# A decoder layer's attention: one of two head pairs has its probabilities parted into f16 and turned by DMA transposes

## The chip, the cores and the metric

One core of a Trainium2 chip runs the whole layer in one launch. The metric is device time in microseconds of one execution, here the median of three runs. The core's engines work from queues of their own and meet at semaphores: TensorE (products and transposes, into PSUM), ScalarE, VectorE, GpSimd, and SyncE, which here only issues DMAs.

## The reference, cut to what matters

The layer has causal self-attention, a cross-attention with three recurrent steps, and a mixture of eight experts. The change is in the first. `x` is (8, 256, 256) in f32, there are 16 heads of 64.

```python
q = (x @ Wq).reshape(N, S, HEADS, HEAD_DIM).transpose(0, 2, 1, 3)
k = (x @ Wk).reshape(N, S, HEADS, HEAD_DIM).transpose(0, 2, 1, 3)
v = (x @ Wv).reshape(N, S, HEADS, HEAD_DIM).transpose(0, 2, 1, 3)
logits = jnp.einsum('nhid,nhjd->nhij', q, k) * scale
causal = 1000000000.0 * (jnp.tril(jnp.ones((S, S), dtype=logits.dtype)) - 1.0)
attn = jax.nn.softmax(logits + causal[None, None, :, :], axis=-1)
out = jnp.einsum('nhij,nhjd->nhid', attn, v)
out = out.transpose(0, 2, 1, 3).reshape(N, S, HEADS * HEAD_DIM)
return out @ Wo + bo
```

## The kernel before, in words

Attention is cut into 32 double steps (STAGES), four to each of the eight batches. A double step has two pairs of heads, p = 0 and p = 1. The projections run as f16 products on operands parted in two: a high half (the value cast to f16) and a low half (what is left), and three products, high x high, high x low and low x high (`HILO`, `split_matmuls`). Scores, the transposes of the probabilities and the weighing of the values are f32. An f32 product of scores and of the weighing shows as two passes in the trace, so 24 rows for 12 products.

All engines run the same loop over j, from -2 to 32, and each has its own fixed order in it. In iteration j TensorE computes the scores of step j+1, weighs the values of step j-1, projects queries and keys of step j+2 (its first pair), does a share of the preparation of the cross-attention, transposes the probabilities of step j (`turn_prob`), projects the output of step j-1, then the second pair of queries and keys (`queries_keys` evicts them) and the values of step j+1. The shares differ: none before j = 8, four transposes from 8 on, f32 products from 18 to 25, four transposes again from 26.

VectorE adds the mask and finds the maxima (`masks`), ScalarE takes the exponentials, GpSimd multiplies by the reciprocal sums (`normalise`), TensorE turns the result in PSUM, and VectorE (pair 0) and ScalarE (pair 1) copy it to `pT` (`probs_turned`). With each step go 36 weight pieces of the experts, a filler for ScalarE (`piece_high`, 2, 1, 2, 0 of them in four iterations), VectorE (`piece_low`, in shares, at three places of an iteration) and SyncE, which loads a piece and stores its halves (`piece_load`, `piece_store`). A buffer holds three pieces. In iterations 4 to 7 ScalarE also squares the context.

SyncE's queue is in the order of the text of `attention_sync`: inputs, attention weights, three pieces, ten context loads, two stores of zeros (`rows_x`, `back_y`), then the loads and stores of the pieces. PSUM bank 1 holds the values of step j until ScalarE has evicted them (`values_out`); then the weighing of step j-1 writes there. That is why the weighing waits for `v_out`.

Of the kernel before, what the change touches and what calls it, by code (L numbers as in the profile page):

```python
# [34 lines left out]
def decoder_layer(nc, a, out):  # L35
# [23 lines left out]
    with top:  # L59
# [58 lines left out]
        def constants_pool():  # L118
# [12 lines left out]
            PO.memset(zrow[:, :], 0.0).then_inc(const_fill, 1)  # L131
# [200 lines left out]
        def vw_tensor(i):  # L332
# [8 lines left out]
            elif i == 1:  # L341
                PE.wait_ge(qk_out, ITEMS)
            elif i < 4:
                PE.wait_ge(pT_out, 2 * STAGES)
            else:
                PE.wait_ge(o_hi, STAGES)
                PE.wait_ge(o_lo, STAGES)
# [109 lines left out]
        p_out = [sem(f"p_out{u}") for u in range(STAGED)]  # L457


        with ExitStack() as c:  # L460
            wo = [sb(c, f"wo{i}", [P, PAIRS, D], F16) for i in range(2)]
            bo = sb(c, "bo", [P, D])
            zrow = sb(c, "zrow", [P, D + 2])
# [17 lines left out]
            w_in = [sem(f"w_in{i}") for i in range(4)]  # L481
            x_in = [sem(f"x_in{i}") for i in range(3)]
# [6 lines left out]
                sem(k) for k in ("recip", "normed", "pT_out", "o_hi", "o_lo"))  # L489
            y_added, y_stat, y_rstd, y_out = (sem(k) for k in ("y_added", "y_stat", "y_rstd", "y_out"))  # L490
# [7 lines left out]
            FIRST, LAST = -2, STAGES  # L498
            X_EARLY = 2
# [103 lines left out]

            def attention_sync():
# [17 lines left out]
                SY.dma_start(rows_x[0:P, :], zrow[:, :]).then_inc(zeroed, 16)  # L622
# [18 lines left out]
            def attention_pool():  # L641
                def normalise(m, p):
                    u = m % 2
                    PO.wait_ge(recip, 2 * m + p + 1)
                    for h in (2 * p, 2 * p + 1):
                        for t in range(2):
                            r = query_tile(t)
                            PO.tensor_scalar(prob[u][:, h, r], prob[u][:, h, r], rden[u][:, h, t:t + 1],  # L648
                                             1.0, ALU.mult, ALU.mult).then_inc(normed, 1)
# [12 lines left out]
                for j in range(FIRST, LAST + 1):  # L662
                    if j >= 0 and j % DOUBLES == 0 and j // DOUBLES < NB:
                        add_bias(j // DOUBLES)
                    if 0 <= j + 1 < STAGES:
                        normalise(j + 1, 0)
                        normalise(j + 1, 1)
                    if batch_ending(j) is not None and j < LAST:
# [10 lines left out]
            def attention_tensor():  # L679
# [13 lines left out]
                def turn_prob(m):  # L693
                    for p in range(2):
                        if m + 1 < STAGES:
                            PE.wait_ge(masked, 8 * (m + 1) + 4 * (p + 1))
                        PE.wait_ge(normed, 8 * m + 4 * (p + 1))
                        for h in (2 * p, 2 * p + 1):
                            for blk in range(3):
                                mm = PE.transpose(ps[:, 2 + h, blk * P:blk * P + P],  # L700
                                                  prob[m % 2][:, h, blk * P:blk * P + P], ident[:, :])
                        mm.then_inc(p_turned, 1)
# [18 lines left out]
                def scores(m):  # L721

                    if m >= 2:
                        PE.wait_ge(pT_out, 2 * (m - 1))
                    for p in range(2):
                        PE.wait_ge(qk_out, 2 * m + p + 1)
                        for t in range(2):
# [6 lines left out]
                def weigh_values(m):  # L734
                    PE.wait_ge(pT_out, 2 * (m + 1))
                    PE.wait_ge(v_out, min(m + 2, STAGES))
                    for p in range(2):
                        for t, key, at in ((0, 0, 0), (1, 0, P), (1, 1, 2 * P)):
                            for h in range(2):
                                r = slice(HD * h, HD * h + HD)  # L740
                                mm = PE.matmul(ps[r, 1, (2 * p + t) * P:(2 * p + t) * P + P], v_sb[m % 2][:, key, p, r],  # L741
                                               pT[:, 2 * p + h, at:at + P], start=key == 0, stop=key == t,
                                               skip_group_check=True)
# [1794 lines left out]
```

## Time and profile before

| | us |
|---|---|
| median of 3 runs | 889.33 |
| lowest, highest | 887.21, 890.68 |
| the profiled execution | 890.64 |
| its span, first to last instruction | 889.4 |
| TensorE busy in the span | 859.9 (97%) |
| VectorE busy | 606.1 (68%) |
| ScalarE busy | 557.2 (63%) |
| GpSimd busy | 377.8 (42%) |

The span is what the trace covers, and its times count from the first instruction. The mean granted TensorE clock is 0.996 of full. The double steps take the time from about 16 to 357 us. In rows of the timeline the first number is the start, the second the time from it to the end of the group, then engine, line, operation, output and input, shape, and the count; in brackets the idle time before and who ended it. TensorE's products overlap, so the start of the next group says more than the length of one.

### The profile page before, as it was taken

What the parts mean: (1) busy time and instruction counts of PE and PEld (TensorE: products, weight loads), DVE (VectorE), ACT (ScalarE), POOL (GpSimd) and SP (SyncE); (2) the same over time, 40 slices, a digit from 0 to 9 for tenths busy, and PEclk for the clock granted to TensorE, in tenths of its full rate; (3) what the DMA queues carried; (4) which work ended last, traced back from release to release, by engine and by line L of the source; (5) the groups of instructions that cost most, each with busy time, mean ns of one, the idle gap of its engine ahead of it and who ended that gap; (6) DMA issues with size and microseconds to landing.
All of it is one profiled execution on the core that took longest, in us unless ns stands there. A gap on an engine that the chain in (4) does not pass through costs nothing. (4 is left out here: it accounts for less than half of the span.)

```text
span 889.4 us, 23089 instructions
## 1 busy us (share of the span) xinstructions
PE 859.9 (97%) x8094; PEld 680.0 (76%) x8094; DVE 606.1 (68%) x1669; ACT 557.2 (63%) x1251; POOL 377.8 (42%) x492
## 2 busy tenths in 40 slices
PE   5999999999999999999999999999999999999996
PEld 3888788888888888767676666676788888887864
DVE  3667588776667675756666667869677767766655
ACT  4988776777676776655756565564455555555555
POOL 1634354343433475324444332544534444444433
PEclk9999999999999999999999999999999999999999
DMA  9733424342424331410000000399423323333226
GB/s 317 207 126 113 142 97 152 119 160 96 143 94 138 103 119 49 62 42 2 1 1 1 2 1 1 105 393 356 158 52 50 49 44 50 49 50 50 43 27 195
DMA packets 61579, 88.04 MB, mean 99 GB/s; under 512 B 17279, under 2 KB 46527, under 8 KB 61343
## 3 DMA queue, kind: packets, MB, share of 16 engines
q1 hardware_dynamic: 53439, 75.52, 25.8%
q0 software_dynamic: 7488, 10.27, 7.3%
q8 instruction: 71, 1.16, 0.6%
q10 hardware_dynamic: 544, 0.79, 0.3%
q14 instruction: 37, 0.30, 0.1%
HBM read 56.00 MB, written 30.56 MB: 97 GB/s over the span
## 5 line engine op out<-in xcount | busy, mean ns | idle before, releaser
L648 POOL TENSOR_SCALAR prob<-prob,rden 128x128 f32<-128x128 f32 (+1 forms) x256 | 122.9, 498 | 183.1 <-DVE rden L949 183.0
L2219 PE MATMUL ps<-slots,e 128*128 128x128 f16 x1872 | 190.0, 219 | 2.2 <-DVE xs L2386 2.1
L2219 PEld LDWEIGHTS ps<-slots,e 128*128 x1872 | 152.6, 97 | 35.3 <-issue 4.4
L843 ACT ACTIVATE prob<-prob,nmx 128x128 f32<-128x128 f32 (+1 forms) x256 | 113.2, 444 | 29.8 <-DVE nmx L943 29.8
L2227 PE MATMUL ps<-e,xT 128*128 x312 | 117.3, 378 | 0.0
L2316 ACT ACTIVATE slots<-slots 128x512 f32<-128x512 f32 x78 | 49.1, 630 | 106.8 <-DVE slots L2370 106.8
L943 DVE CUSTOM_DVE_ANT_0 prob<-ps,mask 128x128 f32<-128x128 f32 (+1 forms) x256 | 73.7, 353 | 41.5 <-PE ps L730 41.5
L31 PE MATMUL ps<-xT,wqkv 128*128 128x256 f16 x768 | 97.2, 278 | 2.0 <-ACT slots L850 1.4
L31 PEld LDWEIGHTS ps<-xT,wqkv 128*128 128x128 f16 x768 | 73.4, 99 | 18.3 <-issue 6.9
L1731 POOL DMA_INDIRECT xg<-rows_x,dst x39 | 40.9, 1049 | 106.3 <-DVE mask L2359 103.0
L2228 PE MATMUL ps<-e,xT 128*128 x312 | 85.0, 273 | 0.0
L2375 DVE TENSOR_TENSOR xT<-slots,xT 128x1024 f16<-128x1024 f32 x39 | 47.8, 1225 | 39.9 <-ACT xT L2322 39.9
L2191 POOL DMA_INDIRECT back_y<-xs,dst x39 | 62.2, 1595 | 29.8 <-DMA back_y<-xs,dst 16.7
L2370 DVE SCALAR_TENSOR_TENSOR slots<-ps,b1e 128x512 f32<-128x512 f32 x78 | 53.7, 691 | 26.5 <-PE ps L2219 26.3
L592 DVE SCALAR_TENSOR_TENSOR parted<-piece,parted 128x256 f16<-128x256 f32 x144 | 59.8, 463 | 0.0
L31 PE MATMUL ps<-an,wqkv 120*128 120x256 f16 x432 | 58.9, 272 | 0.5 <-POOL an L1477 0.5
L730 PE MATMUL ps<-slots 64*128 64x128 f32 (+1 forms) x512 | 53.1, 345 | 2.5 <-ACT slots L850 2.5
L31 PEld LDWEIGHTS ps<-an,wqkv 120*128 120x128 f16 x432 | 41.2, 99 | 16.5 <-POOL an L1477 2.5
L31 PE MATMUL ps<-wst,whh 128*128 128x512 f16 x216 | 52.5, 379 | 0.0
L31 PE MATMUL ps<-s,whh 128*128 128x512 f16 x216 | 52.5, 379 | 0.0
L956 DVE COPY pT<-ps 128x768 f32<-128x768 f32 x32 | 30.6, 956 | 31.8 <-PE ps L700 31.8
L741 PEld LDWEIGHTS ps<-pT,v 128*64 128x64 f32 x768 | 42.4, 139 | 11.5 <-issue 11.5
(267 smaller groups left out, 1855.3 us busy)
## 6 DMA issues: line engine op xcount, KB each, us to landing
halves<-parted SPq DMA_DIRECT2D x36, 512.0 KB, 2.9
piece<-in_L_ffn_ew SPq DMA_DIRECT2D x32, 512.0 KB, 4.5
e<-halves SPq DMA_DIRECT2D x16, 1024.0 KB, 15.2
piece<-in_L_ffn_sh_w SPq DMA_DIRECT2D x4, 512.0 KB, 8.8
sw<-halves SPq DMA_DIRECT2D x4, 512.0 KB, 6.8
rows_x<-xs SPq DMA_DIRECT2D x4, 512.0 KB, 7.4
xs<-back_y SPq DMA_DIRECT2D x8, 256.0 KB, 4.4
out<-xs SPq DMA_DIRECT2D x8, 256.0 KB, 2.1
```

Source lines behind the costliest of these rows:

```text
L31: mm = pe.matmul(out, w, x, start=first and n == 0, stop=last and n == len(products) - 1, **kw)
L592: VE.scalar_tensor_tensor(share(piece_part(q, 1)), share(like_part(q)), WS, share(piece_part(q, 0)), ALU.mult, ALU.subtract).then_inc(p_lo, 1)
L648: PO.tensor_scalar(prob[u][:, h, r], prob[u][:, h, r], rden[u][:, h, t:t + 1], 1.0, ALU.mult, ALU.mult).then_inc(normed, 1)
L730: mm = PE.matmul(ps[:, 2 + 2 * p + h, query_tile(t)], qk[p][r, 0, t * P:t * P + P], qk[p][r, 1, 0:(t + 1) * P], start=True, stop=True)
L843: SC.activation(at, at, ACT.Exp, bias=nmx[u][:, h, t:t + 1], scale=-1.0, accum_out=den[u][:, h, t:t + 1]).then_inc(exped, 1)
L943: VE.tensor_tensor_reduce(prob[u][:, h, r], ps[:, 2 + h, r], mask[:, r], -SCALE, HIGHEST, ALU.add, ALU.min, nmx[u][:, h, t:t + 1]).then_in ...
L2191: PO.indirect_dma_start(back_y, bass.IndirectOffsetOnAxis(ap=dst[:, i:i + 1], axis=0), yo[i % 2], None, compute_op=ALU.add).then_inc(rows_ ...
L2219: yield PE.matmul(ps[:, 2 * u + q, (k % 4) * P:(k % 4) * P + P], w[ch][h], xgT[u][j][:, ch, :], start=n == 0, stop=n == 3 * DC - 1)
L2227: yield PE.matmul(ps[:, 4 + u, :], he[u][0][:, k, :], w, start=k == 0, stop=False, skip_group_check=True)
L2228: yield PE.matmul(ps[:, 4 + u, 0:D], he[u][1][:, k, :], w[:, 0:D], start=False, stop=k == IC - 1, skip_group_check=True)
L2316: SC.activation(z, z, ACT.Gelu_apprx_tanh).then_inc(U_gelu, 1)
L2370: VE.scalar_tensor_tensor(z, ps[:, 2 * u + q, :].rearrange("p (k t) -> p k t", k=4), 1 / WS, bias, ALU.mult, ALU.add).then_inc(U_bias, 1)
```

## The change

The probabilities of pair 0 are no longer turned by TensorE. ScalarE casts them to f16 (`probs_high`, the high half), GpSimd subtracts that from the f32 value (`probs_low`, the low half, times 4096 both), and SyncE issues one DMA transpose of the 128x1536 f16 block into `pT_parts` (`turn_parts`). The values of pair 0 are parted as well: ScalarE writes the high half, VectorE the low one (`values_low`), scaled by 8. TensorE weighs them in three f16 products in place of one f32 product, three key blocks by two heads by three, 18 in all. The heads' eviction divides by 4096 x 8. Pair 1 stays f32 as it was, and its turned probabilities are copied by ScalarE alone. `p_parts`, the source of the transpose, is one buffer; `pT_parts` is two. SyncE's loop is written in the order of the iterations now, with each transpose at the second of three places. `bo`, `zrow`, the f32 values and some semaphores share storage with others.

```diff
@@ PSUM and SBUF
-            v_sb = [sb(c, f"v{i}", [P, S // P, 2, P]) for i in range(2)]
+            v_sb = [v.rearrange("p (k n) -> p k n", n=P) for v in (xg[:, 1, 0:S], part(wst[0], 4 * DC * G3, S))]
+            v_parts = [[sb(c, f"v{i}_{h}", [P, S // P, P], F16) for h in range(2)] for i in range(2)]
-            pT = sb(c, "pT", [P, 4, 384])
+            pT = sb(c, "pT", [P, 2, 384])
+            p_parts = sb(c, "p_parts", [P, 2, 2, 384], F16)
+            pT_parts = [sb(c, f"pT_parts{u}", [P, 2, 2, 3, P], F16) for u in range(2)]
@@ SyncE
+            def turned_parts(engine, m):
+                engine.wait_ge(parts_turned[m % 2], 16 * (m // 2 + 1))
+            def turn_parts(m):
+                SY.wait_ge(prob_lo, m + 1)
+                if m >= 2:
+                    SY.wait_ge(o_mm, m - 1)
+                SY.dma_start_transpose(
+                    out=pT_parts[m % 2][:, :, :, :, :].rearrange("p i h k q -> p (i h k) q"),
+                    in_=p_parts[:, :, :, :].rearrange("p i h n -> p (i h n)")).then_inc(parts_turned[m % 2], 16)
...
-                for q in range(PIECES + STAGED - 1):
-                    if PIECES_EARLY <= q < PIECES:
-                        piece_load(q)
-                    if q >= STAGED - 1:
-                        piece_store(q - STAGED + 1)
+                for j in range(-1, STAGES):
+                    for place in range(3):
+                        if place == 1 and j + 1 < STAGES:
+                            turn_parts(j + 1)
+                        for n in low_shares.get((j, place), ()):
+                            if n % LOW_SHARES == LOW_SHARES - 1:
+                                if n // LOW_SHARES + STAGED < PIECES:
+                                    piece_load(n // LOW_SHARES + STAGED)
+                                piece_store(n // LOW_SHARES)
@@ GpSimd, after normalise(j + 1, 0) and normalise(j + 1, 1)
+                def probs_low(m):
+                    PO.wait_ge(prob_hi, m + 1)
+                    PO.tensor_tensor(p_parts[:, 1, :, :], prob[m % 2][:, 0:2, :], p_parts[:, 0, :, :],
+                                     ALU.subtract).then_inc(prob_lo, 1)
@@ TensorE
-                    for p in range(2):
-                        if m + 1 < STAGES:
-                            PE.wait_ge(masked, 8 * (m + 1) + 4 * (p + 1))
-                        PE.wait_ge(normed, 8 * m + 4 * (p + 1))
-                        for h in (2 * p, 2 * p + 1):
...
+                    PE.wait_ge(normed, 8 * (m + 1))
+                    for h in (2, 3):
...
-                    PE.wait_ge(pT_out, 2 * (m + 1))
                     PE.wait_ge(v_out, min(m + 2, STAGES))
...
+                    PE.wait_ge(v_lo, min(m + 2, STAGES))
+                    turned_parts(PE, m)
+                    for blk, (t, key) in enumerate(((0, 0), (1, 0), (1, 1))):
+                        for n, (i, j) in enumerate(HILO):
+                            for h in range(2):
+                                r = slice(HD * h, HD * h + HD)
+                                PE.matmul(ps[r, 1, t * P:t * P + P], v_parts[m % 2][i][:, key, r],
+                                          pT_parts[m % 2][:, j, h, blk, :], start=key == 0 and n == 0,
+                                          stop=key == t and n == len(HILO) - 1, skip_group_check=True)
+                    PE.wait_ge(pT_out, m + 1)
@@ ScalarE; probs_high(j + 1) stands between the pieces and queries_keys(2 * (j + 2) + 1)
+                def probs_high(m):
+                    SC.wait_ge(normed, 8 * m + 4)
+                    if m >= 1:
+                        turned_parts(SC, m - 1)
+                    SC.copy(p_parts[:, 0, :, :], prob[m % 2][:, 0:2, :]).then_inc(prob_hi, 1)
...
-                    SC.mul(v_sb[m % 2][:, :, :, :], ps[:, 1, :].rearrange("p (t m n) -> p t m n", t=2, m=2),
-                           1 / WS).then_inc(v_out, 1)
+                    SC.mul(v_sb[m % 2], v[:, 1, :, :], 1 / WS).then_inc(v_out, 1)
+                    SC.mul(v_parts[m % 2][0][:, :, :], v[:, 0, :, :], V_UP / WS).then_inc(v_hi, 1)
@@ VectorE; values_low(j) stands first in the iteration, ahead of the masks
-                def probs_turned(m):
-                    VE.wait_ge(p_turned, 2 * m + 1)
-                    if m >= 1:
-                        VE.wait_ge(o_mm, m)
-                    VE.tensor_copy(pT[:, 0:2, :], ps[:, 2:4, 0:384]).then_inc(pT_out, 1)
+                def values_low(m):
+                    VE.wait_ge(v_hi, m + 1)
...
+                    VE.scalar_tensor_tensor(v_parts[m % 2][1][:, :, :], v, V_UP / WS, v_parts[m % 2][0][:, :, :], ALU.mult,
+                                            ALU.subtract).then_inc(v_lo, 1)
```

TensorE's queue before, over iteration 2: scores (L730), weighing (L741), queries and keys, transposes (L700), output projection (wo), queries and keys.

```order
L730 MATMUL ps<-slots 128x128 x2
L730 MATMUL ps<-slots 128x256 x2
L741 MATMUL ps<-pT,v 64x128 x12
L31 MATMUL ps<-xT,wqkv 128x256 x12
L700 MATMUL ps<-ident,prob 128x128 x12
L31 MATMUL ps<-wo,oT 128x256 x12
L31 MATMUL ps<-xT,wqkv 128x256 x12
```

The same place of the changed kernel; v_0 and v_1 are the high and low halves of the values, pT_parts the transposed halves of the probabilities.

```order
L761 MATMUL ps<-slots 128x128 x2
L761 MATMUL ps<-slots 128x256 x2
L773 MATMUL ps<-pT_parts,v_0 64x128 x4
L773 MATMUL ps<-pT_parts,v_1 64x128 x2
L773 MATMUL ps<-pT_parts,v_0 64x128 x4
L773 MATMUL ps<-pT_parts,v_1 64x128 x2
L773 MATMUL ps<-pT_parts,v_0 64x128 x4
L773 MATMUL ps<-pT_parts,v_1 64x128 x2
L780 MATMUL ps<-pT,wst 64x128 x6
L31 MATMUL ps<-xT,wqkv 128x256 x12
L729 MATMUL ps<-ident,prob 128x128 x6
L31 MATMUL ps<-wo,oT 128x256 x12
```

Six transposes of twelve are gone, six f32 products of the weighing stay, and 18 f16 products stand ahead of them. SyncE's queue before, from the last context loads on:

```order
L163 DMA nw<-in_L_xattn_input_norm_w 128x2x1
L163 DMA nw<-in_L_xattn_slot_norm_w 128x2x1
L622 DMA rows_x<-zrow 128x258
L623 DMA back_y<-zrow 128x256
L602 DMA halves<-parted 128x2048
L598 DMA piece<-in_L_ffn_sh_w 128x4x256
```

And of the changed kernel:

```order
L163 DMA nw<-in_L_xattn_input_norm_w 128x2x1
L163 DMA nw<-in_L_xattn_slot_norm_w 128x2x1
L641 DMA rows_x<-xg 128x258
L642 DMA back_y<-xg 128x256
L619 DMA_TRANSPOSE pT_parts<-p_parts 128x12x128 x4
L605 DMA piece<-in_L_ffn_sh_w 128x4x256
L609 DMA halves<-parted 128x2048
```

The transposes of steps 0 to 3 stand behind the context loads and the two stores of zeros, and ahead of the first piece's load. ScalarE's queue around the end of an iteration, before:

```order
L857 COPY pT<-ps 128x768
L582 ACTIVATE parted<-piece 128x1024
L834 ACTIVATE wo<-wst 128x512
L850 ACTIVATE slots<-ps 128x512
L863 ACTIVATE v<-ps 128x512
L843 ACTIVATE prob,den<-prob,nmx 128x128
```

And of the changed kernel (L904 is the high half, L913 and L914 the values):

```order
L897 COPY pT<-ps 128x768
L589 ACTIVATE parted<-piece 128x1024
L874 ACTIVATE wo<-wst 128x512
L904 CAST p_parts<-prob 128x768
L890 ACTIVATE slots<-ps 128x512
L913 ACTIVATE wst<-ps 128x256
L914 ACTIVATE v_0<-ps 128x256
L883 ACTIVATE prob,den<-prob,nmx 128x128
```

The high half stands ahead of the queries and keys (L890), and one eviction of the values has become two.

## Rows read from the trace of the kernel before

**Rows 1.** The page, chain that ended last: share of the span by engine.

```profile
PE 33%; DVE 2%; issue 1%; POOL 1%; ACT 1%; DMA 0%; DVEq 0%; POOLq 0%; ACTq 0%
```

**Rows 2.** Waits from 40 to 345 us: total, times, longest.

```profile
ACT parted L582 <- DMA piece<-in_L_ffn_ew: 6.1, 6, 1.9
...
PE ps L730 <- ACT slots L850: 2.0, 2, 1.8
```

**Rows 3.** Timeline of TensorE, iteration 10: start, length, group.

```profile
125.31 1.58 PE L730 MATMUL ps<-slots 64*128 64x128 f32 x16
126.82 1.53 PE L741 MATMUL ps<-pT,v 128*64 128x128 f32 x24
128.29 1.48 PE L31 MATMUL ps<-xT,wqkv 128*128 128x256 f16 x12
...
130.04 1.47 PE L700 MATMUL ps<-ident,prob 128*128 128x128 f32 x12
131.35 1.47 PE L31 MATMUL ps<-wo,oT 128*128 128x256 f16 x12
132.66 1.47 PE L31 MATMUL ps<-xT,wqkv 128*128 128x256 f16 x12
...
135.38 1.58 PE L730 MATMUL ps<-slots 64*128 64x128 f32 x16
```

**Rows 4.** Timeline of ScalarE, iteration 10.

```profile
125.42 0.60 ACT L863 ACTIVATE v<-ps 128x512 f32<-128x512 f32 x1 [0.67 <-PE ps L31]
126.97 0.40 ACT L843 ACTIVATE prob<-prob,nmx 128x128 f32<-128x128 f32 x1 [0.95 <-DVE nmx L943]
...
130.97 0.57 ACT L850 ACTIVATE slots<-ps 128x512 f32<-128x512 f32 x1
131.55 0.80 ACT L857 COPY pT<-ps 128x768 f32<-128x768 f32 x1
132.25 1.06 ACT L582 ACTIVATE parted<-piece 128x1024 f16<-128x1024 f32 x1
134.17 0.60 ACT L850 ACTIVATE slots<-ps 128x512 f32<-128x512 f32 x1 [0.86 <-PE ps L31]
```

**Rows 5.** Timeline of SyncE's queue, end of the context loads.

```profile
38.53 1.00 SPq L163 DMA_DIRECT2D nw<-in_L_xattn_slot_norm_w  x1
...
40.08 0.43 SPq L623 DMA_DIRECT2D back_y<-zrow  x1
```

**Rows 6.** Timeline of TensorE, first expert tile: products without others between.

```profile
637.75 4.23 PE L2219 MATMUL ps<-slots,e 128*128 128x128 f16 x48
```

**Rows 7.** Timeline of VectorE, first mask of iteration 10.

```profile
126.28 0.29 DVE L943 CUSTOM_DVE_ANT_0 prob<-ps,mask 128x128 f32<-128x128 f32 x1 [0.82 <-PE ps L730]
```

**Rows 8.** Groups of GpSimd: busy us, mean ns, idle before.

```profile
L655 POOL TENSOR_TENSOR xs<-xs,bo 128x512 f32<-128x512 f32 x8 | 10.5, 1308 | 0.0
```

**Rows 9.** Timeline at the start of iteration 1, ScalarE and TensorE.

```profile
31.47 0.58 ACT L850 ACTIVATE slots<-ps 128x512 f32<-128x512 f32 x1
31.84 1.58 PE L730 MATMUL ps<-slots 64*128 64x128 f32 x16
```

**Rows 10.** DMA issues: count, KB each, median us to landing.

```profile
halves<-parted SPq DMA_DIRECT2D x36, 512.0 KB, 2.9
...
bih<-in_L_xattn_gru_bih SPq DMA_DIRECT2D x1, 3.0 KB, 10.0
```

**Rows 11.** Timeline of TensorE, starts of iterations 4, 9, 18 and 26.

```profile
61.16 0.93 PE L730 MATMUL ps<-slots 64*128 64x128 f32 x8
...
114.81 1.58 PE L730 MATMUL ps<-slots 64*128 64x128 f32 x16
...
206.76 1.58 PE L730 MATMUL ps<-slots 64*128 64x128 f32 x16
...
297.56 1.58 PE L730 MATMUL ps<-slots 64*128 64x128 f32 x16
```

**Rows 12.** Busy time and clock (PEclk) of a stretch after the longest stall.

```profile
104.50:107.50 3.00, 3.00 (x28) 2.42 (x24) 1.96 (x11) 1.50 (x8) 0.44 (x2) 0.50 0.00 0
```

More of the change, by code:

```diff
@@ L489, in decoder_layer @@
                 sem(k) for k in ("recip", "normed", "pT_out", "o_hi", "o_lo"))
+            v_hi, v_lo, prob_hi, prob_lo = (sem(k) for k in ("v_hi", "v_lo", "prob_hi", "prob_lo"))
+            parts_turned = [sem(f"parts_turned{u}") for u in range(2)]
             y_added, y_stat, y_rstd, y_out = (sem(k) for k in ("y_added", "y_stat", "y_rstd", "y_out"))
@@ L498, in decoder_layer @@
             FIRST, LAST = -2, STAGES
+            P_UP, V_UP = 4096.0, 8.0
+            O_UP = P_UP * V_UP
             X_EARLY = 2
@@ L693, in turn_prob @@
                 def turn_prob(m):
-                    for p in range(2):
-                        if m + 1 < STAGES:
-                            PE.wait_ge(masked, 8 * (m + 1) + 4 * (p + 1))
-                        PE.wait_ge(normed, 8 * m + 4 * (p + 1))
-                        for h in (2 * p, 2 * p + 1):
[L699 to L702, printed above, removed]
+                    if m + 1 < STAGES:
+                        PE.wait_ge(masked, 8 * (m + 2))
+                    PE.wait_ge(normed, 8 * (m + 1))
+                    for h in (2, 3):
+                        for blk in range(3):
+                            mm = PE.transpose(ps[:, 2 + h, blk * P:blk * P + P],
+                                              prob[m % 2][:, h, blk * P:blk * P + P], ident[:, :])
+                    mm.then_inc(p_turned, 1)
                 def project_qk(n):
@@ L721, in scores @@
                 def scores(m):
-                    if m >= 2:
-                        PE.wait_ge(pT_out, 2 * (m - 1))
+                    if m >= 1:
+                        PE.wait_ge(masked, 8 * m)
                     for p in range(2):
                         PE.wait_ge(qk_out, 2 * m + p + 1)
+                        if p == 1 and m >= 2:
+                            PE.wait_ge(pT_out, m - 1)
                         for t in range(2):
@@ L852, in probs_turned @@
                 def probs_turned(m):
[L854 removed]
+                    SC.wait_ge(p_turned, m + 1)
                     if m >= 1:
                         SC.wait_ge(o_mm, m)
[L857 removed]
+                    SC.copy(pT[:, :, :], ps[:, 4:6, 0:384]).then_inc(pT_out, 1)
+                def probs_high(m):
+                    SC.wait_ge(normed, 8 * m + 4)
+                    if m >= 1:
+                        turned_parts(SC, m - 1)
+                    SC.copy(p_parts[:, 0, :, :], prob[m % 2][:, 0:2, :]).then_inc(prob_hi, 1)
                 def values_out(m):
@@ L870, in heads_high @@
                         SC.wait_ge(y_mm, (b - 1) * SHARES + slot // 2 + 1)
-                    SC.copy(oT[0][:, slot:slot + 2, :].rearrange("p s q -> p (s q)"), ps[:, 1, :]).then_inc(o_hi, 1)
+                    SC.mul(oT[0][:, slot:slot + 2, :].rearrange("p s q -> p (s q)"), ps[:, 1, :],
+                           1 / O_UP).then_inc(o_hi, 1)
                 inputs_high(0)
@@ L1717, in decoder_layer @@
                 sem(k) for k in ("U_mm", "U_bias", "U_gelu", "U_hi", "U_lo", "D_mm", "D_out"))
-            gathered = [sem(f"gathered{q}") for q in range(NT // 2)]
             f_stat, f_rstd, f_norm, f_late, stored = (
@@ L2419, in late_low, with combine_loaded @@
                 VE.tensor_tensor(hh[m % 3][1], hf[m % 2], hh[m % 3][0], ALU.subtract).then_inc(H_late, 1)
+            def combine_loaded(engine, q):
+                engine.wait_ge(loaded[q], 32 if q < len(w_in) + len(x_in) else 16)
             def combine_load(engine, q):
                 rows = back_y[P + q * CT * P:P + (q + 1) * CT * P, :].rearrange("(t p) d -> p t d", p=P)
-                engine.dma_start(xs[:, q * CT:(q + 1) * CT, :], rows).then_inc(gathered[q], 16)
+                engine.dma_start(xs[:, q * CT:(q + 1) * CT, :], rows).then_inc(loaded[q], 16)
             def combine_sync():
```

50 lines of the change are left out of this document (29 added, 21 removed).

## The prediction

> **What bounds the kernel now.** I read the page first, then the waits, then one iteration in order of time. TensorE has 33% of the span in the chain that ended last, the next engine 2% [rows 1]; over the attention stage it waited for another engine only twice [rows 2]. So the 32 double steps cost what TensorE's queue costs. One of them, iteration 10 in the loop over j, runs from 125.31 to 135.38: 10.07 us, of which scores take 1.51, the weighing 1.47 (126.82 to 128.29) and the twelve transposes 1.31 (130.04 to 131.35) [rows 3]. ScalarE in the same iteration starts the values' eviction at 125.42, the first exponential at 126.97, has exponentials and the heads' copy done at 130.97, copies pT, parts a weight piece, and then waits 0.86 us for TensorE [rows 4]. Its idle time is about 3 us in 10, so it is the next engine in line. SyncE's queue is the other place to look at: it is still issuing the context loads when the double steps are under way, and is free only at 40.08 + 0.43 = 40.51 [rows 5].
>
> **The change, part by part.** The profiled run took 890.64 us (span 889.4), 1.3 above the median 889.33; I sum on 890.6.
>
> *TensorE.* Six of twelve transposes go: 1.31 / 2 = 0.655 us per iteration. Of the 24 f32 passes of the weighing 12 stay (0.735). The other 12 become 18 f16 products of 64 columns. Now a pass takes 61 ns (1.47 / 24), since the two heads write different column halves side by side. No f16 product in halves is in the trace. Bounds: 48 f16 products of the same 128 columns over the whole array take 4.23 us, 88 ns each [rows 6]; if halves do not overlap, 18 x 88 = 1.58. An f16 product of 256 columns takes 109 ns (131.35 to 132.66 for twelve) [rows 3], so 128 columns in two halves side by side could go at 27 ns, 0.49 in all. I take 48 ns, a little above 88 halved and below the 61 of the pass that it replaces: 0.87 us. So an iteration bound by TensorE goes from 10.07 to 10.07 - 0.655 - 0.735 + 0.87 = 9.55: a gain of 0.52 (bounds 0.90 and -0.19).
>
> The Trainium skill (TensorEngine Tiling (Array Packing), "Restrictions") says that column tiling switches the fast weight load off. By it the 18 loads would be slower than those of the 128-column products, the cost would lie in the upper half of my bounds, and the gain per iteration would be near zero, which makes the sum some 10 us longer; no row shows such an f16 load, so I leave it in the bounds.
>
> *ScalarE.* It gets the high half of the probabilities, 128x768, and two evictions of 256 columns for one of 512. The 768-element copy of pT occupies it 0.70 us (131.55 to 132.25) [rows 4]; the same for the new one. The two evictions push the parted values' end from 0.6 to about 0.66 after their start, then VectorE needs 0.46 for the low half, all ahead of the masks: these now start 0.86 us after the eviction (126.28) [rows 7], then about 1.15. The first exponential moves from 1.55 to 1.85 after it. With nothing to wait for, an iteration of ScalarE is then 1.85 + 4.00 (exponentials and heads) + 0.48 + 0.70 (pT) + 0.70 (new) + 0.50 (last queries and keys) = 8.23 us, plus 0.96 per weight piece. Pieces per iteration go 2, 1, 2, 0 in turn, the inputs' copy adds 0.48 once in four, and a piece that isn't there yet added 6.1 us over six times [rows 2]. Over four iterations: 32.9 + 4.8 + 0.5 + 0.8 = 39.0 us, against TensorE's 4 x 9.55 + 0.44 = 38.6, and unevenly placed (10.6 beside 10.0, then 11 beside 9.6). I put four at 39.6 instead of 40.7: 0.28 gained per iteration, not 0.52. Behind the new copy in ScalarE's queue stand the queries and keys for which scores wait, so its lateness lands on TensorE at once.
>
> *VectorE* loses the pT copy (0.96) and gains 0.46. *GpSimd* gains a subtraction over 128x768: 1.31 x 768 / 512 = 1.96 us [rows 8], in a queue that idles more than that. Both are covered.
>
> *SyncE and the transfer.* The first transpose, T(0), stands behind all context loads, so it can't be issued ahead of 40.51. Two instructions wait for it: the weighing of step 0, and ScalarE's high half of step 1 (the buffer of parts is single), behind which stand the queries and keys that ran at 31.47 and let the second half of scores go at about 32.6 [rows 9]. No transpose is in the trace. Bounds for issue to landing: 2.9 us for a 512 KB store in large rows, 10.0 for a load in 4-byte elements [rows 10]. The probabilities are 384 KB in 256-byte rows; I take 4.0, near the first. It lands at 44.5; then 0.8 for the high half, 0.6 for queries and keys: scores go on at 45.9 instead of 32.6. Start: **+13.3** (bounds 12.2 and 19.3). Later ones are issued when the low half is done, about 1 us into an iteration, and wanted 6.9 us later by ScalarE (an iteration of 9.7 less 0.7 for the high half, 1.96 for the low one and 0.1): hidden.
>
> The Trainium skill puts a crossbar transpose at 261 GB/s (DMA: Bandwidth & Descriptors, "Latency and other measured facts"), which with the 2 us of fixed cost in its section on the anatomy of one DMA is an estimate of 3.5 us: by it the sum would be 0.5 us less. No run yet shows it.
>
> *The sum by stages* (starts in [rows 3, 9, 11]):
> Start: +13.3.
> Iterations 1 to 3: now 61.16 - 31.84 = 29.3. ScalarE also scales output weights (0.55 each): 3 x 8.23 + 5 x 0.96 + 1.65 + 0.5 + 0.8 = 32.4: +3.1. TensorE's slow clock after the long stall lies beside this.
> Iterations 4 to 8: now 53.65, with the longest stall, 1.8, and a granted clock of 0.50 behind it [rows 2, 12]. ScalarE also squares the context (1.07 in each of four): 9.3 + 11.7 + 10.3 + 13.0 + 9.6 = 53.9, and I add 1: +1.2.
> 9 to 17: 9 x 0.28 = -2.5.
> 18 to 25: 11.35 each ((297.56 - 206.76) / 8), with f32 products of the preparation that leave ScalarE room: 8 x 0.52 = -4.2.
> 26 to 31: 6 x 0.28 = -1.7.
> Together +9.2: **900 us**. Its own range is 892 to 910.
>
> **Rivals.**
> *The transfer is slow.* High half (0.7), low half (1.96), issue (0.1) and landing L follow one another and must fit an iteration of 9.7: it decides from L = 6.9. For it: many short rows; against it: large transfers land in 2.9. With the far row, L = 10.0, a period is 12.8; 31 of them take 397 against 327 now (10.56 each), +70, and the start +19: about 978. The Trainium skill (VectorE: DVE Perf Modes, "The three transpose paths") has 1309 ns for one block of 128x128; twelve in a row would be an estimate of 15.7 us. As a mechanism of this kernel, blocks that go one by one, each double step would take 18.5 us and the time beyond 1100. I give this form 0.05 of the 0.23 below.
> *Loads of pieces come late.* SyncE's queue now holds the load that follows a transpose until the low half is there. For it: the late piece that already stopped TensorE for 1.8 us and was followed by half the clock [rows 2, 12]; against it: such loads have an iteration of slack. Eight such stalls of 1 us more and half of them with the slow clock: +8 + 4 x 1.7 = +15, 915.
> *Not slower.* One mechanism: the side-by-side halves go at 27 ns and ScalarE's idle 3 us takes all that is new, so each of 31 iterations gains 0.90 (28 us), against 12.2 + 1 at the start: 876. It decides from a gain of 0.42 per iteration on. Against it is the ScalarE sum of 39.0 for four. At a gain of 0.4 the time is that of before.
>
> **How the numbers follow.** Forecast 0.48; late pieces 0.12; slow transfer 0.23; not slower 0.17, of it 0.09 faster and 0.08 the same. A difference under 0.5% (4.4 us) is no change for a measurement of this kernel. So faster 0.09, same 0.08, slower 0.83. The range leaves out the gain below 889 and the slowest transfers: 889 to 980.
>
> **What would show it.** Right: TensorE idle for about 13 us from 32.6 on, ended by a DMA or ScalarE; the transpose issued at 40.5; the 18 products in 0.87 us; iterations of about 9.9 from 9 to 17 and 10.8 from 18 to 25. Wrong: a landing above 6.9 us, and TensorE or ScalarE waiting for it in every iteration; products at 88 ns; or a first transpose well ahead of 40 us.

## The result

| | us |
|---|---|
| before, median of 5 runs beside it | 888.42 (886.57 to 890.68) |
| after, median of 5 runs | 948.64 (947.51 to 955.58) |
| ratio | 1.0689, 95% interval 1.0651 to 1.0727 |
| the profiled execution of after, its span | 955.58, 954.3 |
| mean granted clock of TensorE | 0.961 (0.996 before) |

The change costs 60 us. A cost of 10 was forecast, in a range of 889 to 980. The profiled execution is the slowest of the five, 7 us above the median, so the waits and stages read from it below are a little larger than those of a median one.

The page of the changed kernel, busy time of TensorE and the chain that ended last:

```profile
PE 859.9 (90%) x8094; PEld 664.2 (70%) x8094; DVE 595.2 (62%) x1669; ACT 583.1 (61%) x1315; POOL 434.6 (46%) x524
...
PE 30%; DVE 2%; issue 1%; POOL 1%; ACT 1%; DMA 0%; DVEq 0%; POOLq 0%; ACTq 0%
```

TensorE is busy for 859.9 us, to the tenth what it was before. So the whole 64.9 us by which the span grew (889.4 to 954.3) are idle TensorE. That the busy time stays the same hides two things: less work, and a slower clock. The chain has hardly changed [rows 1]: it names TensorE, and doesn't show where the time went. The waits do. From 14 to 430 us (engine, line, what it waited for: total, times, longest):

```profile
POOL p_parts L677 <- ACT p_parts L904: 93.2, 27, 11.5
...
PE ps L761 <- ACT slots L890: 56.9, 15, 13.4
ACT parted L589 <- DMA halves<-parted: 45.4, 24, 3.6
...
ACT p_parts L904 <- DMA pT_parts<-p_parts: 12.7, 1, 12.7
```

Scores wait for queries and keys 56.9 us in 15 stalls. The same line of the kernel before, over the same stretch:

```profile
PE ps L730 <- ACT slots L850: 2.5, 3, 1.8
```

So 54.4 of the 64.9 us are this wait. One of the stalls is the start, 13.4. The others go with a wait that the kernel before did not have: ScalarE, about to write the high half of a weight piece into `parted`, waits for the *store* of the piece that was there, 24 times.

The DMA issues (KB each, median us from issue to landing):

```profile
halves<-parted SPq DMA_DIRECT2D x36, 512.0 KB, 5.6
...
pT_parts<-p_parts SPq DMA_TRANSPOSE x32, 3.8
```

Transposes land in 3.8 us. The stores land in 5.6, where they took 2.9 [rows 10].

Starts of iterations in both traces [rows 11 for before] give the time by stages:

| iterations | before | after | longer | forecast |
|---|---|---|---|---|
| 1 to 3, with the start | 29.32 | 46.17 less 0.87 (earlier begin) | 16.0 | 16.4 |
| 4 to 8 | 53.65 | 70.78 | 17.1 | 1.2 |
| 9 to 17 | 91.95 | 106.40 | 14.5 | -2.5 |
| 18 to 25 | 90.80 | 99.85 | 9.1 | -4.2 |
| 26 to the end | 591.84 | 600.13 | 8.3 | -1.7 |

The first stage is as forecast; the error lies in the 28 iterations behind it. Iterations of 9.9 us from 9 to 17 and of 10.8 from 18 to 25 were to show that the prediction was right; they take 11.8 and 12.5. Here is one such place in four engines' own order (start, length, group, in brackets the idle time before it and what ended it). SyncE's queue while TensorE is in iterations 7 and 8:

```profile
121.52 1.42 SPq L619 DMA_TRANSPOSE pT_parts<-p_parts  x1
122.98 0.89 SPq L605 DMA_DIRECT2D piece<-in_L_ffn_ew  x1
123.91 0.44 SPq L609 DMA_DIRECT2D halves<-parted  x1
124.40 0.43 SPq L605 DMA_DIRECT2D piece<-in_L_ffn_ew  x1
124.87 1.34 SPq L609 DMA_DIRECT2D halves<-parted  x1
137.61 1.42 SPq L619 DMA_TRANSPOSE pT_parts<-p_parts  x1
```

VectorE's low halves; a piece has four shares, and the first two of these four complete the piece that is stored at 123.91:

```profile
114.69 1.49 DVE L599 SCALAR_TENSOR_TENSOR parted<-piece,parted 128x256 f16<-128x256 f32 x4
```

ScalarE:

```profile
126.33 0.78 ACT L897 COPY pT<-ps 128x768 f32<-128x768 f32 x1
129.60 1.06 ACT L589 ACTIVATE parted<-piece 128x1024 f16<-128x1024 f32 x1 [2.49 <-DMA halves<-parted]
133.15 1.06 ACT L589 ACTIVATE parted<-piece 128x1024 f16<-128x1024 f32 x1 [2.49 <-DMA halves<-parted]
...
135.05 0.81 ACT L904 CAST p_parts<-prob 128x768 f16<-128x768 f32 x1
135.77 0.59 ACT L890 ACTIVATE slots<-ps 128x512 f32<-128x512 f32 x1
```

GpSimd, then TensorE:

```profile
135.94 1.64 POOL L677 TENSOR_TENSOR p_parts<-prob,p_parts 128x768 f16<-128x768 f32 x1 [7.17 <-ACT p_parts L904]
```

```profile
136.41 1.65 PE L761 MATMUL ps<-slots 64*128 64x128 f32 x8 [6.27 <-ACT slots L890]
```

Read it as a ring. The piece was complete at about 115.4 (two of four shares, 114.69 + 0.73). Its store could have gone then, but SyncE stood at the transpose, which goes at 121.52 only, and then had the load ahead of the store; so the store goes at 123.91, 8.5 us late, and lands at 129.52. ScalarE wants the buffer at 127.1, gets it at 129.60, waits again, and its high half starts at 135.05 instead of about 130 (two pieces and the squares behind 127.1). GpSimd has been idle 7.17 us for that. Its low half ends at 137.6, and only then SyncE issues the next transpose, at 137.61. Each store behind it is late again: the lateness of one iteration is handed to the next. The slow landing has a part in it too: with the 2.9 us of the kernel before, the store issued at 123.91 would have landed by 126.8, an estimate, just in time. Meanwhile TensorE stands 6.27 us. During the stall its granted clock falls to half, from 132.5 to 142.7. Columns are length, busy us (instructions) of PE, PEld, DVE, ACT, POOL, then the clock:

```profile
136.40:140.40 4.00, 3.99 (x39) 3.01 (x40) 3.40 (x20) 2.37 (x10) 2.42 (x2) 0.50 0.44 83
```

All stretches at 0.50 (1.2 of 2.4 GHz) sum to 75.9 us, against 8.3 before; each sum has 4 to 6 us at the very end of the run in it, where TensorE does nothing. TensorE is not busy in all of them. The sum over the ten stretches ahead of the end:

```profile
sum 71.67, PE 50.32 PEld 37.30 DVE 42.39 ACT 46.55 POOL 34.49; mean PE 5.03 PEld 3.73 DVE 4.24 ACT 4.66 POOL 3.45
```

Before, TensorE was busy for 3.4 us at half clock. So the slow clock adds (50.3 - 3.4) / 2 = 23.5 us to its busy time, an estimate that takes each busy us at 0.50 for half a us of work.

### The profile page after: what moved, and what is told of

The parts are those of the page before. It is cut to its first block and busy times, and to the rows that moved or that the text cites. A ratio compares the mean times of both kernels' runs of the same rounds, so it can differ in the third digit from the quotient of the medians.

```text
span 954.3 us, 23279 instructions
## 1 busy us (share of the span) xinstructions
PE 859.9 (90%) x8094; PEld 664.2 (70%) x8094; DVE 595.2 (62%) x1669; ACT 583.1 (61%) x1315; POOL 434.6 (46%) x524
## 5 line engine op out<-in xcount | busy, mean ns | idle before, releaser
L671 POOL TENSOR_SCALAR prob<-prob,rden 128x128 f32<-128x128 f32 (+1 forms) x256 | 126.8, 504 | 109.4 <-DVE rden L1003 98.4
L761 PE MATMUL ps<-slots 64*128 64x128 f32 (+1 forms) x512 | 61.5, 372 | 57.0 <-ACT slots L890 56.9
L31 PE MATMUL ps<-xT,wqkv 128*128 128x256 f16 x768 | 102.8, 288 | 2.4 <-ACT slots L890 1.8
L677 POOL TENSOR_TENSOR p_parts<-prob,p_parts 128x768 f16<-128x768 f32 x32 | 52.9, 1652 | 93.2 <-ACT p_parts L904 93.2
L761 PEld LDWEIGHTS ps<-slots 64*128 64x128 f32 x512 | 37.7, 202 | 71.7 <-ACT slots L890 64.3
L2429 DVE TENSOR_TENSOR xT<-slots,xT 128x1024 f16<-128x1024 f32 x39 | 47.8, 1226 | 39.6 <-ACT xT L2376 37.6
L1010 DVE SCALAR_TENSOR_TENSOR v<-ps,v 128x256 f16<-128x256 f32 x32 | 13.5, 422 | 94.0 <-ACT v L914 94.0
L589 ACT ACTIVATE parted<-piece 128x1024 f16<-128x1024 f32 x36 | 37.9, 1058 | 45.4 <-DMA halves<-parted 45.4
```

The lines of the kernel that those rows point to most:

```text
L31: mm = pe.matmul(out, w, x, start=first and n == 0, stop=last and n == len(products) - 1, **kw)
L677: PO.tensor_tensor(p_parts[:, 1, :, :], prob[m % 2][:, 0:2, :], p_parts[:, 0, :, :], ALU.subtract).then_inc(prob_lo, 1)
L761: mm = PE.matmul(ps[:, 2 + 2 * p + h, query_tile(t)], qk[p][r, 0, t * P:t * P + P], qk[p][r, 1, 0:(t + 1) * P], start=True, stop=True)
```

## The experiments

The wait total of a row is that of scores for queries and keys, from 14 to 430 us, in the profiled execution; "half clock" is the sum of the stretches granted at 0.50 there. The row of the changed kernel has both from its execution of 955.6 us, so a part of its distance from e1 and e4 in these two columns is that of the execution.

| kernel | ratio to before, 95% | us | wait | half clock |
|---|---|---|---|---|
| before | 1 | 888.4 | 2.5 | 8.3 |
| after | 1.069 (1.065 to 1.073) | 948.6 | 56.9 | 75.9 |
| e1, store ahead of load | 1.065 (1.062 to 1.068) | 947.9 | 49.7 | 67.8 |
| e4, first transposes among the context loads | 1.064 (1.061 to 1.067) | 945.9 | 51.1 | 59.5 |
| e7, high half ahead of the pieces | 1.038 (1.036 to 1.041) | 922.8 | 36.0 | 43.1 |
| e2, transpose behind the pieces' DMAs | 1.032 (1.028 to 1.036) | 917.4 | 30.7 | 37.3 |
| e10, pieces' DMAs from ScalarE | 1.030 (1.027 to 1.033) | 914.2 | 29.2 | 29.4 |
| e5 = e1 + e2 + e4 | 1.016 (1.013 to 1.019) | 904.7 | 19.9 | 29.6 |
| e6 = e5, context loads behind T(0) | 1.011 (1.009 to 1.013) | 898.6 | 14.4 | 26.0 |
| e8 = e6 + e7 | 1.005 (1.004 to 1.007) | 893.6 | 13.7 | 18.3 |
| e13 = e8 + e10 | 1.019 (1.016 to 1.021) | 905.6 | 21.3 | 20.3 |
| e11 = e8, pieces dealt later | 1.023 (1.020 to 1.026) | 908.9 | 21.7 | 23.3 |
| e9, before with load ahead of store | 1.006 (1.004 to 1.008) | 894.5 | 7.3 | 12.7 |
| e12, before, pieces dealt later | 1.034 (1.032 to 1.036) | 919.9 | 24.0 | 36.4 |

**Order of SyncE's queue.** The edits of e1, e2 and e4:

```diff
 # e1
-                                if n // LOW_SHARES + STAGED < PIECES: piece_load(n // LOW_SHARES + STAGED)
                                 piece_store(n // LOW_SHARES)
+                                if n // LOW_SHARES + STAGED < PIECES: piece_load(n // LOW_SHARES + STAGED)
 # e2
                     for place in range(3):
-                        if place == 1 and j + 1 < STAGES: turn_parts(j + 1)
...
+                    if j + 1 < STAGES: turn_parts(j + 1)
 # e4
-                context_loads()
+                context_loads(0, 6); turn_parts(0); context_loads(6, 8); turn_parts(1); context_loads(8, NLOAD)
```

> Changed kernel, but SyncE issues the store of a piece ahead of the next load instead of behind it. Theory A (ScalarE waits for stores because SyncE issues them late: most of the lateness is the transpose's wait in front of them, about 7 us, and about 1 us is the load): each of the 24 waits gets about 1 us shorter, ScalarE's wait for the stores falls from 45 to 20 to 30 us, time 920 to 935. Rival B (the stores land late because the transposes crowd the DMA engines, 5.6 us instead of 2.9): the order changes little, 943 to 950. Rival C (ScalarE's added work is the bound): no change, 948.

> Changed kernel, but in SyncE's program each transpose stands behind all piece stores and loads of its iteration instead of ahead of those of the second and third place. Theory A: the stores go out some 7 us earlier, ScalarE's wait for them falls under 8 us, the stalls of 4 to 6 us in every fourth iteration and the halved clock behind them go: 885 to 900, with the start's 13 us still there. Rival B (crowded DMA engines): stores still land after 5 us and more, the wait stays above 20 us, time above 920. Rival C: 945 or more.

> Changed kernel, but the first two transposes stand ahead of the last four context loads and the stores of zeros in SyncE's queue. Theory A: the stall of 13.4 us in iteration 1 goes, with the half clock of 13.7 us behind it, and the later stalls stay: 948 less 13 to 20, so 928 to 935. Rival (the DMA engines are full of context loads at that time and the transpose lands late anyway): less than 5 us gained, 943 or more.

e1 missed (920 to 935 was expected): it changes as good as nothing, the intervals overlap. By its time alone the two rivals, crowded DMA engines and a full ScalarE, fit as well; the runs below decide. The 45.4 us of waits for stores turn into 36.9 us of waits for loads, the stores landing in 3.9 us. Both stand behind the transpose, so as long as it is ahead of them their own order matters little. The waits of e1:

```profile
ACT parted L589 <- DMA piece<-in_L_ffn_ew: 36.9, 20, 2.9
```

e2 is right in direction, and gives half of the loss back (31 us), 17 to 32 short of what was expected. In e2 stores still land in 5.2, as the rival of crowded DMA engines said, but ScalarE's wait for them falls to 14.2, where that rival had more than 20.

e4 missed too, and came out where its rival had it: the start's stall shrinks from 13.4 to 10.2 only. There the first transpose is issued at 27.93 and holds SyncE for 9.60 us among the context loads.

> All three orders together: stores ahead of loads, transposes last in an iteration, the first two transposes ahead of the slow context loads. Theory A, with the measured 0.5 us for the 18 products (TensorE saves 0.89 us per iteration): TensorE could give 890 less 28, but ScalarE's 39 us for four iterations against 40.7 before allow less: 868 to 882, so faster than the kernel before. Rival C (ScalarE's work bounds): 888 to 900. Rival B: above 905.

> e5_all_order, but the first transpose stands ahead of all ten context loads, the second ahead of the last five. In e5 the first transpose was issued at 28.9 us and landed only at 40.8, with the large context loads in flight. Theory A2 (the remaining 8.1 us stall at the start is the queue of bytes in front of the transpose): the transpose lands about 4 us after its issue, the stall of TensorE goes to under 2 us and with it a stretch of half clock: 904.7 less 8 to 11, 894 to 897. Rival (the first transpose is slow by itself, or code loading): no change, 903 to 906.

Together they give back 44 us, far less than expected (868 to 882), and with the context loads behind T(0) 50, 1.6 us short of the range. In e5 the first transpose, put among those loads, held SyncE for 8.85 us, in e6 it goes ahead of them. SyncE's queue in e5:

```profile
28.93 8.85 SPq L619 DMA_TRANSPOSE pT_parts<-p_parts  x1
```

**The ring cut at ScalarE, and at the queue.** e7 moves one call; e10 issues the pieces' loads and stores from ScalarE, `pieces_moved` standing behind `values_out` and behind the second exponentials.

```diff
 # e7, ScalarE
                         probs_turned(j)
+                    if 0 <= j + 1 < STAGES: probs_high(j + 1)
                     for q in high_at.get(j, ()): piece_high(q)
...
-                    if 0 <= j + 1 < STAGES: probs_high(j + 1)
 # e10
+                    pieces_moved((j - 1, 1), (j - 1, 2))   # piece_store(q, SC), piece_load(q + STAGED, SC)
...
+                    pieces_moved((j, 0))
```

> Changed kernel, with one thing moved: ScalarE makes the high half of the probabilities before the weight pieces of the iteration, not behind them. SyncE's order as in the change (transpose ahead, load ahead of store, start unchanged). Theory A (a ring: a piece waits for its store, the store stands behind the transpose, the transpose waits for the high half, the high half stands behind the piece): the ring is cut, stores go out 2 to 4 us earlier, ScalarE's wait for them falls from 45 to below 20, time 905 to 925. Rival D (only SyncE's order counts, the ring adds nothing): within 5 us of the change, 944 to 952.

> e6_context_later with the high half ahead of the pieces too. Theory A2: what is left of ScalarE's lateness is its own load of 8.2 us and 0.96 per piece, and VectorE's 4 pieces behind GpSimd's subtraction; the high half early lets GpSimd subtract while VectorE is not parting pieces: 3 to 8 us less than e6, 887 to 893, so the same as the kernel before or a little faster. Rival C (ScalarE's work is the bound, whatever the order): as e6, 894 to 897.

> The changed kernel, but the loads and stores of the weight pieces are issued by ScalarE (at the head of an iteration and behind its second exponentials), so that SyncE's queue holds transposes alone after the start. Everything else, the high half behind the pieces included, is as in the changed kernel (948). Theory (the ring goes through SyncE's queue: a store stands behind a transpose that waits for the low half, which waits for ScalarE's high half, which stands behind the piece that waits for the store): the ring is gone, ScalarE waits for stores under 10 us instead of 45.4, TensorE waits about 25 instead of 56.9, the start keeps its 13.3, time 910 to 922, about what cutting the ring at ScalarE gave (922.8). Rival (the transposes slow the transfers themselves: stores land 5.6 us after issue instead of 2.9, whatever queue issued them): waits for stores stay above 25 us, time above 935.

e7 changes nothing on SyncE, and takes 26 us away, as expected: the transpose no longer waits for the piece that waits for the store. Its stores land as late as before the edit (5.7), so these 26 us are not the price of slow landings; 20.9 us of waits for stores are left. e8 lies between its two theories, 0.6 us above the one and 0.4 below the other. e10 leaves the high half where it was, and takes 34 away, as expected. Its waits:

```profile
PE ps L765 <- ACT slots L894: 29.2, 10, 13.6
ACT p_parts L908 <- DMA pT_parts<-p_parts: 13.0, 1, 13.0
ACT parted L589 <- DMA piece<-in_L_ffn_ew: 11.3, 7, 2.8
```

And its DMA issues:

```profile
halves<-parted ACTq DMA_DIRECT2D x36, 512.0 KB, 3.1
```

No wait for a store is left, and 13.6 of the 29.2 us are the start. As many transposes move as many bytes beside the pieces as in the changed kernel, so contention of the transfers (the rival) does not make the waits for stores. One thing is not separated: e10 also has each store ahead of its load. With the transposes ahead that was worth 1 us (e1); with the transposes out of the way it can be worth more (5.5 us in e9, below), so of the 34 us a part may be the order's and not the queue's. e13 shows that two cures don't add up:

> The version with all four orders put right (893.6), and in addition the pieces' loads and stores issued by ScalarE instead of SyncE. Theory (with the transposes last and the high half early the queue costs almost nothing more): 892 to 896, ScalarE waits for loads (3.6 us) unchanged or a little more, because an issue from ScalarE comes up to half an iteration after the low halves are done. Rival (SyncE's queue is still what holds the rest): 889 or less.

It missed both ways, 12 us slower than e8. Its transposes land in 5.8 instead of 4.9, its loads in 5.6 instead of 4.5, and ScalarE waits 6.9 us for loads instead of 3.6. ScalarE's queue also has the issues themselves, some 30 us in all (36 stores of 0.33, 32 loads of 0.45 at the median, 1.8 at most), partly beside its other work. Which of these costs most stays open.

**Pieces without transposes.** Two edits of the kernel before. e9 exchanges load and store in SyncE's loop as the change does; e12 deals the pieces out later (and e11 does the same in e8).

```diff
 # e9
-                    if PIECES_EARLY <= q < PIECES: piece_load(q)
-                    if q >= STAGED - 1: piece_store(q - STAGED + 1)
+                    if q + STAGED < PIECES: piece_load(q + STAGED)
+                    piece_store(q)
 # e11, e12
-            LOW_FROM = 2
+            LOW_FROM = 6    # and one share more at places 1 and 2 where 18 <= j < 26
```

> The kernel before with the one exchange that the change made besides the transposes: the next load of a piece goes ahead of the store of the last. Theory A: harmless by itself, since no transpose holds them back: 888 to 892. Rival E (the exchange delays stores behind 512 KB of load and alone makes ScalarE wait for them): 895 to 915, stores landing after 5 us.

> The version with all four orders put right (893.6) and the pieces dealt out otherwise: from iteration 6 on instead of 2, and one share more at two places of each of the iterations 18 to 25, where ScalarE and VectorE have room. Theory (what is left against the kernel before is iterations 1 to 8, where ScalarE is 74.5 us busy in 92.5, and 18 to 25 gain): the pieces leave five iterations of the first stage at 0.96 us each plus their transfers; the first stage falls from 92.5 to about 88, the later one keeps most of its gain, time 887 to 891. Rival (the start alone sets the loss, the pieces lie in ScalarE's idle time): within 1.5 us of 893.6. Rival (the later iterations are full too): above 895.

> The kernel before with the same dealing of pieces (from iteration 6, more in 18 to 25), as the control for the one beside it. It has 3 us in 10 idle on ScalarE and few waits, so both theories expect little: 886 to 889, no more than 3 us gained from the late piece (1.8 us of waiting and half the clock behind it).

e9: the exchange alone makes stores land in 5.2 instead of 2.9, brings the same wait, and costs 5.5 us, more than the theory (888 to 892) and just less than its rival (895 to 915) had. Its waits:

```profile
ACT parted L582 <- DMA halves<-parted: 12.7, 6, 3.5
```

e12 was meant as a control that moves nothing, and was wrong by 31 us. It shows the price of late pieces in a kernel with no transposes: all of it lies in iterations 18 to 25, which take 121.6 us instead of 90.8. ScalarE:

```profile
279.25 1.06 ACT L583 ACTIVATE parted<-piece 128x1024 f16<-128x1024 f32 x1 [8.05 <-DMA piece<-in_L_ffn_ew]
...
299.50 1.06 ACT L583 ACTIVATE parted<-piece 128x1024 f16<-128x1024 f32 x1 [7.47 <-DMA piece<-in_L_ffn_ew]
```

TensorE right behind them:

```profile
280.84 1.65 PE L731 MATMUL ps<-slots 64*128 64x128 f32 x8 [6.65 <-ACT slots L851]
...
301.10 1.65 PE L731 MATMUL ps<-slots 64*128 64x128 f32 x8 [6.07 <-ACT slots L851]
```

Here the loads are late, since these iterations ask for seven shares on average instead of five, more than three buffers brought. 31.5 us of waits on ScalarE become 24.0 on TensorE and 31.5 in the time; the rest is the half clock, which lengthens TensorE's busy time from 859.9 to 867.6. In the changed kernel 45.4 us of waits for stores and the start's 12.7 go with 56.9 on TensorE.

**What is left in e8.** Iterations 1 to 8, 9 to 17 and 18 to 25 of e8, columns as above:

```profile
33.30:125.80 92.50, 79.72 (x813) 63.10 (x812) 51.23 (x221) 74.45 (x218) 48.69 (x80) 0.94 0.66 166
125.80:218.10 92.30, 87.64 (x949) 73.22 (x948) 69.66 (x267) 76.30 (x220) 57.20 (x88) 0.98 0.65 166
218.10:304.00 85.90, 84.58 (x847) 67.68 (x846) 61.13 (x232) 69.42 (x198) 48.87 (x77) 1.00 0.62 161
```

Before took 82.97, 91.95 and 90.80 us for them. In the last stage, where ScalarE has room, 4.9 us are gained. In the middle one TensorE works 4.3 us less (91.95 before) and gains nothing. In the first, with ScalarE busy for 74.5 us (66.7 before), 9.5 are lost.

e11 took the pieces out of the first of these stages. Its total missed by 18 us (887 to 891 was expected), but its stages tell the two effects apart; the same three stretches of e11:

```profile
33.22:118.03 84.81, 77.05 (x814) 61.38 (x813) 48.52 (x201) 69.45 (x213) 48.48 (x80) 0.98 0.50 119
118.03:209.41 91.38, 86.27 (x949) 72.02 (x948) 69.42 (x267) 76.01 (x220) 57.28 (x88) 1.00 0.67 168
209.41:312.89 103.48, 89.75 (x846) 70.22 (x845) 69.00 (x248) 72.99 (x202) 49.12 (x77) 0.95 0.59 169
```

With pieces dealt from iteration 6 on instead of 2 the first stage takes 84.8 us instead of 92.5, 1.8 above the kernel before; there the same removal gave 0.9 (82.97 to 82.09, e12). So the pieces, which fitted beside the work of this stage before, no longer do. Whether it is ScalarE's time, VectorE's or the transfers that is short was not separated. The last stage takes 103.5 instead of 85.9, with late loads as in e12. No version was faster than the kernel before.

## Why the prediction was wrong

*What bounds the kernel:* right for the kernel before, and right that behind ScalarE's queries and keys its lateness lands on TensorE at once. In the double steps of the changed kernel it is not TensorE's work that sets the time but the ring.

*Start, +13.3:* right. The stall ended by queries and keys is 13.38 us; T(0) was issued at 40.02 (40.5 forecast), landed in about 3.9, and the high half went at 43.90.

*Transposes removed, f32 passes kept:* right. *The 18 f16 products:* 0.87 forecast, from 97.47 to 97.99 measured, 0.52 us:

```profile
97.47 0.69 PE L773 MATMUL ps<-pT_parts,v 128*64 128x128 f16 x18
97.99 0.82 PE L780 MATMUL ps<-pT,xg 128*64 128x128 f32 x12
```

That is 29 ns each, near my lower bound (27). The chosen 48, near the pass that it replaces, was too dear. By the sum's other terms TensorE's work then falls by 0.87 us per iteration, not 0.52; measured, its busy time in e8 falls by 0.78 in each of the iterations 18 to 25 ((90.80 - 84.58) / 8, full clock in both). The right price made the forecast no better, since TensorE was not what waited last.

The weight loads of these products, then a group of 128-column loads for comparison (busy us, mean ns, idle before):

```profile
L773 PEld LDWEIGHTS ps<-pT_parts,v 128*64 128x64 f16 x576 | 21.1, 126 | 22.5 <-issue 17.9 <-ACT xg L913 3.1 <-ACT wst L913 1.5
L31 PEld LDWEIGHTS ps<-wqkv,xT 128*128 128x128 f16 x384 | 37.6, 98 | 4.3
```

A load of 64 columns took 126 ns in the mean (110 at the median), longer than one of 128 columns. With what the Trainium skill says of column tiling and the fast weight load (TensorEngine Tiling (Array Packing), "Restrictions") this agrees. The cost that the prediction drew from it, products in the upper half of the bounds, did not come: the 18 loads lie beside each other and beside the products, from 97.47 for 0.53 us in all.

*Landing of the transposes:* 4.0 forecast, 3.8 measured (longest 5.5); the rival with 10.0 is dead, and so are blocks that go one by one. The 3.5, an estimate worked out from the Trainium skill (DMA: Bandwidth & Descriptors), was nearly as near; the 2 us of fixed cost in it the page gives for DMAs that GpSimd issues, and this one is issued by SyncE.

*GpSimd:* 1.96 forecast, 1.65 measured; *the high half:* 0.70 forecast, 0.72 from start to next start. *VectorE:* 0.46 forecast for the low half of the values, 0.42 measured.

*ScalarE, four iterations at 39.6:* nothing of the changed kernel shows it, since the ring covers it. In e8, where the ring is gone (its queues are in another order, so this is a comparison and no test), iterations 9 to 17 take 92.30 / 9 = 10.26 us, 41.0 for four, so my sum was 1.4 short and the gain of 0.28 per iteration isn't there; about half of the 1.4 is one stretch of half clock, 3.3 busy us of it. The sum itself took 0.48 for the first eviction of queries and keys, where its row has 0.58 (130.97 to 131.55 [rows 4]). 18 to 25 take 85.90 / 8 = 10.74, forecast 10.83. That also speaks against the rival *Not slower*: even with the products at 29 ns and the ring gone, the kernel gains nothing over 9 to 17.

*SyncE, "Later ones are issued when the low half is done ... hidden":* **this is the step that failed.** The transposes are hidden, as it says; what stands behind them in the queue is not. The sum asked only when a transpose lands and who wants it. It didn't ask what SyncE holds back while it waits for the low half: the stores that free `parted`. Nor did it follow the wait backwards: the low half wants the high half, which stands in ScalarE's queue *behind* the pieces that want those stores. It is worth up to 34 us at the queue (e10) or 26 at ScalarE (e7), with all orders of the queue 50 (e6), and with both 55 of the 60 (e8).

*The rival "Loads of pieces come late", 0.12, 915:* the nearest in mechanism (by its number the slow transfer, 978, was nearer, for a reason that did not come true), and wrong in two ways. It named loads, whose slack of an iteration was true of the load's own wait but not of the store that the change put behind it: the diff shows `piece_load` ahead of `piece_store`, and the prediction gave that exchange no price. It costs 5.5 us even without transposes (e9). And it priced eight stalls of 1 us, where there were 14 behind the start with 43.5 us (56.9 - 13.4). The half clock behind them I had priced at 1.7 us each for half of them, 6.8 in all; it adds 23.5 us to TensorE's busy time. As the busy time did not move, the work itself fell by about as much, 23.5 / 32 = 0.73 us per iteration, near the 0.78 of e8. That the two balance to the tenth is chance.

The measured time lies inside the stated range; that is luck. The upper part of the range stood there for transfers of up to 10 us, and the transfers took 3.8.

## What to carry to other kernels

When a DMA that must wait is put into a queue in program order, price what stands behind it: for each later issue ask which buffer it frees, who wants that buffer, and whether the awaited result itself stands behind that wanting in another engine's queue. If it does, it is a ring, and each iteration inherits the lateness of the last; cutting it at one place (here one call moved, 26 us, or another queue, 34) can be worth far more than a sooner landing (stores in 3.9 instead of 5.6 in e1, 1 us). Of two DMAs on one queue, the store that frees a buffer went better first (e9, 5.5 us). And when a total misses, split it by stages: e11 lost 15 us in all and still settled the question that it was built for.

## What the runs showed of the hardware

- An f16 product of 128 columns on half of the array's columns, with another head's on the other half, took 29 ns, 18 in a row. Over the whole array 48 of 128 columns took 88 each [rows 6], and twelve of 256 columns 109 each [rows 3]. The weight loads for 64 columns took 110 ns at the median, those for 128 columns 98.
- A DMA transpose of 384 KB held SyncE's queue for 1.42 us at its issue, in the rows above a load of a piece for 0.43 or 0.89 and a store for 0.44 or 1.34; among the context loads the transpose held it for 8.85 us (e5).
- A 512 KB store landed in 2.9 us when issued ahead of a 512 KB load and in 5.2 behind it (e9), nothing else changed.
- TensorE was busy in 50.3 of the 71.7 us granted at half clock ahead of the run's end; the clock's price was 23.5 us of busy time and not half of 71.7.
- Four shares of pieces on VectorE took 1.49 us, but 2.87 when GpSimd subtracted the low half beside them (63.12 to 64.88, in e5), the row below. One of the four, 1.87 us long and ending 0.28 behind the subtraction, has the whole difference. In the kernel before, one share beside GpSimd's addition of the bias (143.97, 1.43 us) took 1.49 by itself.

```profile
62.96 2.87 DVE L599 SCALAR_TENSOR_TENSOR parted<-piece,parted 128x256 f16<-128x256 f32 x4
```
